# A masked attention's mask products in 64-row halves with a bf16 mask, six of its tiles in borrowed memory

## The reference

```python
scores = q @ k.T * scale                       # per head: 2048 queries x 1601 keys
scores = where(mask == 0, NEG_INF, scores)     # mask: int32, 2048 x 1601
x = layernorm(x + softmax(scores) @ v @ Wo + bo)
```

## Time and profile before

| | before |
|---|---|
| median of 3 runs | 2999.99 us (2996.73 to 3009.27) |
| the profiled execution, its time | 3006.59 us |
| its span, first to last instruction | 3004.8 us |
| TensorE busy | 2786.9 us, 93% |
| VectorE busy | 2157.4 us, 72% |
| ScalarE busy | 1822.5 us, 61% |
| GpSimd busy | 544.2 us, 18% |
| the masked attention phase | about 577 to 1340 us of the span; its loop over heads 645 to 1313 us |
| granted TensorE clock, mean | 0.952 of full speed |

### The profile page before, as it was taken

How to read it: one execution, slowest core, us unless ns; L and a number is a source line. 1 busy time by engine, 2 the same in 40 slices (tenths; PEclk the granted TensorE clock), 3 DMA queues, 4 the chain that set the end, 5 groups by cost and what they waited for, 6 DMA issues and landing times. The chain is left out here.

```text
span 3004.8 us, 93752 instructions
## 1 busy us (share of the span) xinstructions
PE 2786.9 (93%) x39186; PEld 1029.0 (34%) x39187; DVE 2157.4 (72%) x5870; ACT 1822.5 (61%) x2158; POOL 544.2 (18%) x760
## 2 busy tenths in 40 slices
PE   4999999999999999976999999999999999899998
PEld 2622222522222222233322223563222222256664
DVE  7689887488888788746798895227999999652114
ACT  2288878536667666753488887323878877931222
POOL 0188880120000000001222212303000000002330
PEclk7899999979999999997999999997999999989999
DMA  3344441311100111011211111102122221112112
GB/s 98 115 123 133 129 121 42 110 29 26 26 20 20 26 27 26 20 27 41 75 42 41 43 42 49 53 20 66 25 53 69 62 56 33 36 59 65 43 44 87
DMA packets 120407, 166.79 MB, mean 56 GB/s; under 512 B 38228, under 2 KB 89311, under 8 KB 119985
## 3 DMA queue, kind: packets, MB, share of 16 engines
q1 hardware_dynamic: 102192, 117.21, 14.4%
q0 software_dynamic: 12320, 43.02, 4.8%
q10 hardware_dynamic: 5472, 0.56, 0.2%
HBM read 126.51 MB, written 26.72 MB: 51 GB/s over the span
## 5 line engine op out<-in xcount | busy, mean ns | idle before, releaser
L747 DVE TENSOR_REDUCE mpart<-ps 128x1 f32<-128x512 f32 x1536 | 980.3, 683 | 115.2 <-PE ps L555 111.3
L555 PE MATMUL ps<-stack 48*32 48x512 f16 (+6 forms) x13312 | 952.1, 354 | 35.7 <-DVE mpart L747 12.2
L480 ACT ACTIVATE xT<-ps,exp_scale 128x1024 f32<-128x1024 f32 (+3 forms) x800 | 793.7, 1029 | 261.8 <-PE ps L594 121.5
L480 ACT ACTIVATE cn<-ps,exp_scale 128x1024 f32<-128x1024 f32 (+4 forms) x800 | 742.0, 960 | 212.8 <-PE ps L576 99.1
L576 PE MATMUL ps<-stack 50*32 50x512 f16 (+3 forms) x11648 | 756.2, 377 | 64.1 <-ACT xT L480 46.6
L555 PEld LDWEIGHTS ps<-stack 48*32 48x32 f16 x13312 | 282.4, 91 | 1015.5 <-DVE mpart L747 506.0
L740 DVE CUSTOM_DVE_ANT_0 scrap<-ps,arena 128x401 bf16<-128x401 f32 (+1 forms) x1024 | 534.3, 574 | 128.1 <-PE ps L555 128.1
L616 PE MATMUL ps<-xT,vall 128*17 128x512 f32 (+4 forms) x3648 | 421.3, 523 | 2.2 <-POOL xT L439 1.4
L616 PE MATMUL ps<-cn,vall 128*17 128x512 f32 (+3 forms) x3392 | 412.1, 507 | 1.0 <-ACT cn L480 1.0
L576 PEld LDWEIGHTS ps<-stack 50*32 50x32 f16 x11648 | 189.0, 90 | 215.1 <-ACT xT L480 115.7
L734 DVE CUSTOM_DVE_ANT_0 scrap<-ps,scrap 128x128 bf16<-128x128 f32 (+3 forms) x512 | 247.3, 484 | 16.7 <-PE ps L555 12.5
(11 more groups left out here) (282 smaller groups left out, 2548.8 us busy)
## 6 DMA issues: line engine op xcount, KB each, us to landing
stack<-q_parts SPq DMA_DIRECT2D x384, 64.0 KB, 2.7
stack<-k_parts SPq DMA_DIRECT2D x192, 64.0 KB, 2.8
wbuf<-in_maskT POOLq DMA_DIRECT2D x24, 512.0 KB, 4.4
arena<-in_moe_w SPq DMA_DIRECT2D x19, 512.0 KB, 4.6
stack<-k_parts SPq DMA_DIRECT2D x192, 50.0 KB, 2.3
stack<-sums_inverse SPq DMA_DIRECT2D x16, 512.0 KB, 5.6
parts<-osb SPq DMA_DIRECT2D x240, 32.0 KB
wbuf<-in_mask POOLq DMA_DIRECT2D x16, 401.0 KB, 3.8
```

Source lines behind the costliest of these rows:

```text
L480: nc.scalar.activation(e.prob[tile % P_SLOTS][0:rows, half * HALF + first:(half + 1) * HALF], S_PS(g)[0:rows, first:HALF], ACT.Exp, scale= ...
L555: last = nc.tensor.matmul(bank[quarter(j), i * w:i * w + w], qs[b][rows, at:at + 32], ks[b][rows, a:a + w], start=True, stop=True)
L747: nc.vector.tensor_reduce(dst, src, AX, ALU.max).then_inc(unit_used, 1)
```

## The change

- `HOME_TILES` and `AWAY_TILES` name six key tiles each, of the 12 full ones. The transposed mask of a full tile is bf16 now, 2048 columns, in another layout: partitions 0 to 63 hold what bank 0 of a slot needs, partitions 64 to 127 what bank 1 needs, each the 64 lower and then the 64 upper keys of the tile by the 512 queries of that bank. In `mask_scores` the products of bank 0 contract over partitions 0 to 63, those of bank 1 over 64 to 127. The 65-row tile stays fp8 and over its full rows (`e.mask_end`).
- A bf16 mask takes twice the memory. The home tiles lie in `arena`. The away tiles are made first, in the same place, and stored to DRAM (`masks_away`, 6 x 512 KB); the home tiles then overwrite them.
- In the masked phase the biased residual is stored to DRAM (`residual_away`, 2 MB), four away tiles are loaded over it, and two over the weights in `wbuf`. Once tile 7 of the last head is masked, the residual is loaded back; `open_totals` waits for it.
- GpSimd's bias additions move ahead of the values' shift in the masked phase, since the store waits for them.
- In the preparation a full piece of the transposed mask is fetched by two transfers (64 partitions each) instead of one, and compared straight into bf16 by one operation instead of two.

```diff
--- before.py
+++ after.py
 MASKED = -float(2 ** 30)
...
 PAIR_TILES = (2 * S + (NE - 1) * (P - 1)) // P
+HOME_TILES, AWAY_TILES = (0, 1, 2, 3, 8, 9), (4, 5, 6, 7, 10, 11)
 FIRST_SEMAPHORE, PHASE_SEMAPHORES = 142, 56
...
             mask_chain, mask_in = sem("mask_chain"), [sem(f"mask_in{i}") for i in range(2)]
+            masks_stored = sem("masks_stored")
+        if masked:
+            residual_out, residual_in = sem("residual_out"), sem("residual_in")
+            masks_in = [sem(f"masks_in{i}") for i in range(2)]
         if select:
...
                     sp.dma_start(w_out[:, c, :], projection[c * P:(c + 1) * P].rearrange("(h d) o -> d h o", d=HD)).then_inc(o_weights_in, 16)
+                if masked:
+                    sp.wait_ge(biased, NT)
+                    sp.dma_start(e.residual_away, residual.rearrange("p t c -> p (t c)")).then_inc(residual_out, 16)
+                    sp.wait_ge(residual_out, 16)
+                    for t in AWAY_TILES[0:4]:
+                        sp.dma_start(e.mask_tile[t], e.masks_away[AWAY_TILES.index(t)]).then_inc(masks_in[0], 16)
                 place_max(0)
+                if masked:
+                    sp.wait_ge(front_made, len(front))
+                    for t in AWAY_TILES[4:6]:
+                        sp.dma_start(e.mask_tile[t], e.masks_away[AWAY_TILES.index(t)]).then_inc(masks_in[1], 16)
                 for h in range(H):
...
                 load_inverse(1)
+                if masked:
+                    sp.wait_ge(s_ready, (H - 1) * ns + 2 * AWAY_TILES[3] + 2)
+                    sp.dma_start(residual.rearrange("p t c -> p (t c)"), e.residual_away).then_inc(residual_in, 16)
                 for half in range(2):
...
                 if masks_ahead:
-                    sp.wait_ge(mask_chain, 4 * NT + 8 * NT2)
+                    sp.wait_ge(mask_chain, 4 * NT + 4 * (NT2 - 1) + 8)
+                    sp.wait_ge(masks_stored, 16 * len(AWAY_TILES))
                 first = 0 if scale_next is None else 4
...
                 pool.wait_ge(ahead_in, 16 * len(ahead))
+
+                def add_bias(t):
+                    nc.gpsimd.tensor_tensor(residual[:, t, :], e.x_nat[:, t, :], e.b_row, ALU.add).then_inc(biased, 1)
+
+                if masked:
+                    for t in range(NT):
+                        add_bias(t)
                 if v_bias:
...
                                                 shift[0:n], ALU.add).then_inc(v_shifted, 1)
-                def add_bias(t):
-                    nc.gpsimd.tensor_tensor(residual[:, t, :], e.x_nat[:, t, :], e.b_row, ALU.add).then_inc(biased, 1)
-
-                if not select:
+                if not select and not masked:
                     pool.wait_ge(exp_done, 1)
...
                     pieces = []
+                    of_rows, of_keys = tiles(S2, -(-S2 // 4)), tiles(S, CH)
+                    for t in AWAY_TILES:
+                        pieces += [("maskT", t, P, of_keys[0:2]), ("maskT", t, P, of_keys[2:4])]
                     for t in range(NT):
-                        wide = tiles(S2, -(-S2 // 4))
-                        pieces += [("mask", t, P, wide[0:2]), ("mask", t, P, wide[2:4])]
-                        if t < NT2:
-                            wide = tiles(S, CH)
-                            pieces += [("maskT", t, min(P, S2 - t * P), wide[0:2]), ("maskT", t, min(P, S2 - t * P), wide[2:4])]
+                        pieces += [("mask", t, P, of_rows[0:2]), ("mask", t, P, of_rows[2:4])]
+                    first_home = len(pieces)
+                    for t in HOME_TILES:
+                        pieces += [("maskT", t, P, of_keys[0:2]), ("maskT", t, P, of_keys[2:4])]
+                    pieces += [("maskT", NT2 - 1, S2 - (NT2 - 1) * P, cut) for cut in (of_keys[0:2], of_keys[2:4])]
                     stages = [e.mask_stage[:, i * HALF:(i + 1) * HALF] for i in range(2)]
-                    read_by = []
+                    read_by, landed, landed_of = [], [0, 0], []
...
                             pool.wait_ge(mask_chain, read_by[i - 2])
-                        nc.gpsimd.dma_start(stages[i % 2].bitcast(I32)[0:rows, 0:end - start],
-                                            e.d[name][t * P:t * P + rows, start:end]).then_inc(mask_in[i % 2], 16)
+                        stage, rows_of_it = stages[i % 2].bitcast(I32), e.d[name][t * P:t * P + rows, start:end]
+                        if name == "mask" or rows < P:
+                            nc.gpsimd.dma_start(stage[0:rows, 0:end - start], rows_of_it).then_inc(mask_in[i % 2], 16)
+                            landed[i % 2] += 16
+                        else:
+                            for g in range(2):
+                                nc.gpsimd.dma_start(stage[g * ROWS:(g + 1) * ROWS, 0:2 * CH].rearrange("p (k n) -> p k n", k=2),
+                                                    rows_of_it[:, g * CH:(g + 1) * CH].rearrange("(k p) n -> p k n", k=2)
+                                                    ).then_inc(mask_in[i % 2], 16)
+                                landed[i % 2] += 16
+                        landed_of.append(landed[i % 2])
...
                             fetch(i + 1)
-                        pool.wait_ge(mask_in[i % 2], 16 * (i // 2 + 1))
+                        pool.wait_ge(mask_in[i % 2], landed_of[i])
+                        if i == first_home:
+                            pool.wait_ge(masks_stored, 16 * len(AWAY_TILES))
                         for a, n in cut:
...
                                                                    ALU.is_equal, ALU.mult))
+                            elif rows == P:
+                                home = AWAY_TILES.index(t) if t in AWAY_TILES else HOME_TILES.index(t)
+                                chain.link(nc.gpsimd.tensor_scalar(e.mask_home[:, home, a:a + n], stage.bitcast(I32), 0.0, None,
+                                                                   ALU.is_equal))
                             else:
                                 chain.link(nc.gpsimd.tensor_scalar(stage, stage.bitcast(I32), 0.0, None, ALU.is_equal))
-                                chain.link(nc.gpsimd.tensor_copy(e.mask_one[0:rows, t, a:a + n], stage, saturate=False))
+                                chain.link(nc.gpsimd.tensor_copy(e.mask_end[0:rows, a:a + n], stage, saturate=False))
                         read_by.append(chain.n)
+                        if t in AWAY_TILES and name == "maskT" and cut[-1][0] + CH == S:
+                            home = AWAY_TILES.index(t)
+                            nc.gpsimd.dma_start(e.masks_away[home], e.mask_home[:, home, :]).then_inc(masks_stored, 16)
                 if select:
...
                     g = h * ns + n
+                    if n == 2 * AWAY_TILES[0] and h == 0:
+                        pe.wait_ge(masks_in[0], 16 * 4)
+                    elif n == 2 * AWAY_TILES[4] and h == 0:
+                        pe.wait_ge(masks_in[1], 16 * 2)
                     for bank in range(2):
-                        lo, hi = bank * CH, (bank + 1) * CH
+                        lo, hi, at = bank * CH, (bank + 1) * CH, bank * ROWS
                         for j in range(-(-rows // 32)):
-                            last = nc.tensor.matmul(S_PS(g)[quarter(j), lo:hi], e.big16[0:rows, quarter(j)],
-                                                    e.mask_one[0:rows, kt, half * HALF + lo:half * HALF + hi],
-                                                    start=False, stop=True)
+                            if rows < P:
+                                last = nc.tensor.matmul(S_PS(g)[quarter(j), lo:hi], e.big16[0:rows, quarter(j)],
+                                                        e.mask_end[0:rows, half * HALF + lo:half * HALF + hi],
+                                                        start=False, stop=True)
+                                continue
+                            own, of_keys = at + 32 * (j % 2), half * HALF + j // 2 * CH
+                            last = nc.tensor.matmul(S_PS(g)[quarter(j), lo:hi], e.big16[at:at + ROWS, own:own + 32],
+                                                    e.mask_tile[kt][at:at + ROWS, of_keys:of_keys + CH], start=False, stop=True)
                     last.then_inc(s_ready, 1)
...
                 pe.wait_ge(biased, NT)
+                if masked:
+                    pe.wait_ge(residual_in, 16)
                 pe.wait_ge(unit_used, H * nu)
...
         e.xd, e.yd = dr("tokens", (S, D), F32), dr("pairs_out", (2 * S, D), F32)
+        e.masks_away, e.residual_away = dr("masks_away", (len(AWAY_TILES), P, S), BF16), dr("residual_away", (P, NT * D), F32)
         e.sd, e.rd = dr("sums", (H, S), F32), dr("sums_inverse", (H, S), F32)
...
         at = NT * S2 // 2
-        e.mask_one = arena[:, at:at + NT2 * S // 4].bitcast(FP8).rearrange("p (t n) -> p t n", t=NT2)
+        homes = len(HOME_TILES) * S // 2
```

(7 more changed lines are left out.)

## The result

The changed kernel takes 2963.03 us (median of four runs, 2950.18 to 2971.35); the kernel before, run beside it, 3000.05 (four runs, 2996.73 to 3009.27). The ratio is 0.9868, with a 95% interval of 0.9826 to 0.991. It is faster, but by 37 us, not by the 90 that were predicted, and 2963 lies above the upper end of the range, 2942. The profiled execution took 2971.35 us (span 2969.6), 35.2 less than that of before.

What follows compares the result with a forecast made beforehand. TensorE was taken to bound the masked phase, busy 41.96 of 42.20 us a head. 85.5 us from 15 heads plus 6.5 from the last, less 2 for trips, gave 90.0 off 2999.99: 2910.0 us, range 2886 to 2942.

Steps and rivals of the forecast that it cites:

- (1): Masked loop: mask products in two 64-row halves stream together, a group falling from 0.44 to 0.23 us, 5.2 us a head.
- Rival C: Mask products: halves don't stream together, groups stay at 0.44 us, only switches go; 2963 us, chance 0.03.
- (5): Around the masked phase: DRAM store and loads cost 0 to 8 us, residual's way back 0 to 4; 2 taken for both.
- rival E: Round trips show: 8 us at the front, 4 at the end, 2 from the preparation; 2922 us, chance 0.05.
- step (3): Masked heads: VectorE's 33.85 us beside TensorE's 34.6 gives 36.5 us a head (35.5 to 37.5), a gain of 5.7.
- halves and switches: Masked loop: 5.2 us a head from half-row mask products, 2.4 from fewer array-shape changes; TensorE's need 42.2 to 34.6.
- Rival A: Masked loop: VectorE goes hungry around each product, waiting 0.3 us in each of 13 tiles; head 38.2, time 2936, chance 0.22.
- Rival B: Masked phase: all falls into place, no low-clock spells, 35.0 us a head, nothing lost at the ends; 2885 us, chance 0.12.
- Rival D: Masked phase: slower by the clock, half speed for half the time, 60 us more than now; 3060 us, chance 0.02.
- Clock: Masked phase: spells at 1.2 GHz, granted clock a few hundredths under 1.00; cost left in the head's upper bound of 37.5.
- Last head: Masked phase's last head, without units: ScalarE sets it, 27.4 us instead of 33.9, a gain of 6.5.
- Preparation: L0's self-attention, where masks are made: POOL's idle time covers the added work; 0 us, bounds -3 and +3.

Runs made afterwards that it cites:

- run 5: Changed kernel with each masked maximum taken over half of its columns, TensorE's products all kept: 2883.72 us (one run).
- run 6: Kernel before the change with each masked maximum taken over half of its columns: 2976.47 us (one run).
- run 8: Changed kernel with two PSUM banks instead of three for the masked phase's maxima: 3074.69 us (one run).
- run 1: Changed kernel with the mask products moved directly behind the scores, ahead of the units: 2932.25 us, ratio 0.9763.
- run 2: Kernel before the change with the mask products moved directly behind the scores, ahead of the units: 3046.31 us, ratio 1.0152.

## Why the prediction was wrong

**Right.** (1) *Mask in halves*: a group costs 0.23 from start to start between 64-row groups and 0.33 ahead of the product, as forecast; the last head shows both, with no units between:

```profile
1262.91 0.41 PE L620 MATMUL ps<-stack 50*32 50x512 f16 x8
1263.14 0.40 PE L648 MATMUL ps<-arena,big 64*32 64x512 bf16 x8
1263.38 0.41 PE L620 MATMUL ps<-stack 50*32 50x512 f16 x8
1263.61 0.40 PE L648 MATMUL ps<-arena,big 64*32 64x512 bf16 x8
1263.94 1.05 PE L669 MATMUL ps<-cn,vall 128*17 128x512 f32 x8
```

These answer. The 0.46 in the middle of the loop (952.66 to 953.12) is no other price: there the mask's first half starts beside a unit that still has its 0.17 to run, and 952.62 to 953.12 is 0.17 + 0.23 + 0.10. Rival C, whose 2963 happens to be the measured time, is refuted by these rows. (5) *The trips*: both are hidden. SP's rows of the store, the loads and the residual's way back, and the end of the phase on TensorE:

```profile
620.77 0.59 SPq L344 DMA_DIRECT2D residual_away<-x_nat  x1
627.76 1.77 SPq L347 DMA_DIRECT2D x_nat<-masks_away  x4
646.33 0.58 SPq L285 DMA_DIRECT2D max_parts<-mturn  x1
...
1262.06 0.34 SPq L374 DMA_DIRECT2D x_nat<-residual_away  x1
...
1274.89 1.05 PE L669 MATMUL ps<-cn,vall 65*17 65x512 f32 x8 [0.47 <-ACT cn L524]
1275.87 1.13 PE L675 MATMUL ps<-x_nat,ident 128*128 128x512 f32 x2
```

The bias additions end at 620.2 (609.23 and 10.99), 7.5 later than my 612.7, which is the preparation's loss. The loads are issued 18.6 us ahead of the maxima, the store took at most 7.0 us where I had 11, the way back landed 7.7 us after its issue, 6 us ahead of the totals, and the totals stand right behind the last product. The maxima are at 646.33 instead of 638.72, but this is the preparation's 7.4 us. The 2 us counted for the trips weren't needed: the stretch ahead of the first scores is 0.2 us longer than before's. With that rival E is out, apart from the preparation.

**Wrong: step (3), what is late next.** I bounded the coupling of the two engines by the unmasked phase, 1.6 to 2.95 us a head over the fuller engine, and took 36.5. Measured are 39.5. By runs 5 and 6 the 3.0 us fall apart in two. 0.4 are TensorE's own need, 35.0 for 34.6: of the 7.6 us for halves and switches 6.2 came (0.4 of the difference are longer waits for ScalarE, the other 1.0 no run explains), but 1.0 of before's 42.2 had been waits for VectorE, not need, and that made up for most of it. That the 34.6 came out nearly right is so in part luck: I had read before's 41.96 us of busy time as TensorE's need. The other 2.6 are the coupling: 4.5 us over TensorE's need where my 36.5 had room for 1.9.

The unmasked phase was no measure, because its reserve is as long as its hole. Its units have 512 columns, and VectorE takes 0.63 us for each; there are no mask products beside the product. Two products of an unmasked head:

```profile
2272.80 4.39 DVE L802 TENSOR_REDUCE mpart<-ps 128x1 f32<-128x512 f32 x7
...
2273.54 0.40 PE L599 MATMUL ps<-stack 48*32 48x512 f16 x4
2273.87 1.05 PE L669 MATMUL ps<-xT,vall 128*17 128x512 f32 x8
2274.85 0.40 PE L599 MATMUL ps<-stack 48*32 48x512 f16 x4
...
2276.05 0.30 PE L599 MATMUL ps<-stack 48*32 48x65 f16 x16
...
2277.10 0.42 DVE L800 TENSOR_REDUCE mpart<-ps 128x4 f32<-128x260 f32 x1
...
2277.71 0.69 DVE L802 TENSOR_REDUCE mpart<-ps 128x1 f32<-128x512 f32 x1 [0.19 <-PE ps L599]
```

4.39 / 7 = 0.63. At 2273.54, the last unit ahead of the first product, VectorE has its operation of 2273.43 and two more, 1.77 us; the unit behind the product starts at 2274.85 and can be read 0.45 later, a hole of 1.76. So VectorE goes through without a stop, seven operations in a row. At the second product the last unit is a short one, which takes 0.42 to read, and 0.19 are lost. In the masked phase it is 1.43 against 1.89. The two numbers that decide could be read from before, in the order of one product:

```profile
941.55 0.35 PE L555 MATMUL ps<-stack 48*32 48x401 f16 x4
...
942.89 0.08 DVE L740 DVE_READ_ACCUMULATOR2_ANT mpart<- 128x1 f32 x1
...
943.64 0.58 DVE L740 CUSTOM_DVE_ANT_0 scrap<-ps,arena 128x401 bf16<-128x401 f32 x1 [0.66 <-PE ps L555]
```

The hole was 2.09 us there (941.55 to 943.64), the reserve 1.42 (to 942.97), the wait 0.66; the 13 waits of a head made 8.3. The change makes the mask group in the hole 0.21 shorter and leaves the reserve: 13 x 0.21 = 2.7 us, a head of 39.5. That this meets the measured 39.5 to the tenth is luck in part: the waits fell by 2.2, and VectorE's busy time, which I would have left alone, by 0.5.

**Rival A** named this mechanism ("VectorE goes hungry around each product"), with mask group, switch and product as 1.3 us. That is the second fault: the hole runs from the last unit's start, not its end, to the start of VectorE's next operation. 0.17 of the unit ahead and 0.40 from the next unit's start to its reader were left out, which makes 1.3 into 1.87. Its 0.3 us did not even follow from its own 1.3 against 1.5. The wait came out as 0.46 in each of 13 tiles: 33.35 + 6.1, and the head as 39.5 where the rival had 38.2. And the chance of 0.22 was too low. The row that spoke for it, 5.7 us of idle time already in before, 8.3 over all maxima, was read as a wait that costs nothing. It cost 1.0 us a head even there (run 6); once TensorE has time to spare, most of the wait is on the path, 4.5 of the 6.1 us in after (run 5). The Trainium skill (TensorEngine Tiling (Array Packing), "PSUM Bottleneck") has the warning that tiling speeds up TensorE and not the reading of PSUM; runs 5 and 8 agree, 35.0 us a head with lighter reads and 46.3 with one bank less.

Rival B asked for 35.0 us a head: TensorE could do it, as run 5 shows, and VectorE's ring kept it from it. Rival D (slower, by the clock) has nothing for it.

**Clock.** I expected spells at a lower clock in the masked phase, as in the unmasked one, and they stayed out: 1.00 in the middle head, with TensorE busy for 37.83 of 39.50 us, while an unmasked head has 0.91 at 33.70 of 36.70, and another 1.00 at 30.90 of 33.30. In the head with 0.91 the clock falls to its lower level (0.50, 1.2 GHz) at 2401.2; from 2391.2 to there TensorE was busy for 9.22 us and never stood idle for more than 0.27. The Trainium skill (TensorE: Matmul & The Clock Gate, "Loop structure matters more than you think"), which calls dense work safe, was right for this phase; it was I who set it aside. Why the clock falls in the unmasked phase no run here shows. The cost that I had left in for them hid some of the error: without it the sum would have been further off.

**Last head.** 29.5 us against 27.4. I had a tile as TensorE's 1.98 us, less than two exponentials. One tile takes 2.01 (1262.91 to the next one's scores at 1264.92), the next 2.40 (to 1267.32), since a score group in it comes 0.40 late, for an exponential. The engines take turns here too: TensorE is busy for 26.70 and ScalarE for 26.35 of the 29.50 us, and neither alone sets the time.

**Preparation.** I took 0, with bounds of 3 us either way; 7.4 were lost in the profiled execution, and between 2.0 gained and 5.3 lost in the others with this preparation or its spread form. They go along with the granted clock; the cause stays open. An average over 300 us (10 GB/s more) can't show what single stretches of 10 us at a share of 1.0 do.

## What to carry to other kernels

Where two engines pass work through n banks, read two times: the reserve, n times the reader's start to start less what has run of the operation in hand, and the hole, from the start of the writer's last item ahead of its long foreign work to the reader's start on the next one. Where the hole is longer, the reader idles by the difference in each round however much of its time is free on average, and making the writer faster elsewhere gives only what this ring lets through. Don't take the writer's busy time for its need: waits can lie under it, and a run with a lighter reader shows how much (runs 5 and 6). Take short work out of the hole first (run 1: -1.8 us a head), and take care that the move adds no change between array shapes (run 2: +2.9).
